# Gate product, sum and statistics of the attention block by halves in earlier slots, x's statistics four slots later

## The chip, the cores and the metric

The kernel runs on one core of one Trainium2 chip. The metric is the device time of one execution in microseconds, as the median of several runs.

## What is computed

Sixteen graphs of 512 tokens with 256 features go through one attention layer and one expert layer, both with a residual. Cut to what matters here:

```
x = x + gnn(layernorm(x), adj)        # statistics of x
x = x + ffn(layernorm(x))             # statistics of x1
gnn(x):  q, k, v = x Wq', x Wk', x Wv'            # 8 heads of 32
         c = softmax(where(adj, q k' / sqrt(32), -inf)) v
         gate = sigmoid([c, x] Wg' + bg)
         return gate * x + (1 - gate) * c
ffn(x):  two of 8 experts by the router's top 2, plus one shared expert
```

With z = tanh of half the gate's argument, gate is (z + 1)/2, so the layer's output is x1 = x + c + 0.5 (z + 1)(xn - c), where xn is the normalised x. The kernel computes `diff` = xn - c and x1 = x + c on GpSimd, then on VectorE the *gate product* diff = (z + 1) * diff and the *sum* x1 = 0.5 * diff + x1. x1's statistics follow, then its normalisation for the expert layer.

## The kernel before

**Stages.** The attention block goes through the 16 graphs (batches), software-pipelined over three of them: while batch b is in attention, b + 1 is normalised and projected ("pre") and b - 1 is gated and finished ("post"); b - 2 is routed ("late"). A program of 32 slots makes a batch. In each slot every engine has one score tile (128 queries of one head by 512 keys): TensorE computes the scores (L480), VectorE adds the mask and takes the maximum into `pf` and `nmax` (L836), one slot later ScalarE takes the exponent (L609), three slots later TensorE transposes it (L490), four later ScalarE copies it to `pt` (L597), and twelve slots later, for eight tiles together, TensorE multiplies with v (L511).

**Units.** Beside the tiles, `UNIT_AT` (L24) gives TensorE a unit of other work in a slot: V0, V1 (values), C0, C1 (transposes of the attention's output `c_tok`), R0 (router positions), Z0 to Z3 (gate, one of the four token tiles of 128 each), P0, P1 (transposes of the normalised xn), Q and K (projections), X0, X1 (transposes of the normalised x1). ScalarE evacuates the unit's high part in the next slot, VectorE the low part a slot after that (`low`: L697 for P, L700 for Q and K, L702 for C, L708 for V). Z units are evacuated by ScalarE alone, a tanh into a quarter of `z`.

**Order.** Every engine's order is written out by these tables and is static. `DVE_AT` (L29) sets VectorE's slots for the rest: `stat` and `var` are the four statistics of x and their aggregation (L732, L738, L740), `gate` is the gate product (L875), `x1` the sum (L880), `stat2` (two token tiles in the slot named and two in the next) and `var2` the same for x1. `POOL_AT` sets GpSimd's: `diff` and `x1` in slots 8 and 10, x's reciprocal deviation and normalisation in 12 and 13 (L936, L941), and from slot 17 on eight indirect DMAs (L923) that scatter batch b - 2 to the experts' rows. SP's queue stores the normalised xn (L370) and then x1 (L376), and then sends the stacks of q and k for the next scores.

**Waits that matter.** Scores have two banks, `S`, so those of slot p wait until VectorE is done with tile p - 2. Transposes wait for the exponent of their own tile and for the copy of two tiles before. Z0 to Z3 wait for both low parts of C before their second half. GpSimd's normalisation waits for `var`'s result `vr` on VectorE, and its scatters stand behind that in its queue.

**Behind the attention.** From the last batches on, TensorE interleaves the slots with the shared expert's blocks (`seam`); then come 35 routed blocks.

Of the kernel before, what the change touches and what calls it, by code (L numbers as in the profile page):

```python
# [12 lines left out]
ALU = mybir.AluOpType  # L13
# [12 lines left out]
HALVES = "QKV"  # L26

ACT_AT = {"exp": 5}
DVE_AT = {"choose": 3, "mark": 4, "weigh": 6, "place": 14, "stat": 8, "var": 12, "bias0": 4, "bias1": 16, "gate": 19,  # L29
          "x1": 20, "stat2": 21, "var2": 23}  # L30
POOL_AT = {"diff": 8, "x1": 10, "rstd": 12, "xn": 13, "rstd2": 24, "xn2": 25}
SCATTER_AT = {17: [0, 1], 18: [2, 3], 19: [4], 20: [5], 21: [6], 22: [7]}

# [32 lines left out]
def attention_phase(nc, sems, held, banks, x, adj, wqkv, wgate, bg, router_w, xn_dram, x1_dram, xt2_dram, xg_dram,  # L66
# [7 lines left out]
    NB, N, D = x.shape  # L74
# [18 lines left out]
    if True:  # L93
# [171 lines left out]
        def unit(b, name):  # L265

            return (b + 1) * NU + ORDER.index(name)
# [38 lines left out]
        def sync(sp):  # L306
# [53 lines left out]
            def end(b):  # L360
                par, att, pre, post = flags(b)
                B = b + 1
                A = b - 1
                if pre:
                    sp.wait_ge(s_bias, B * 2 + 1)
                    sp.dma_start(adj_i[:, :, :], (adj_t[B] if isinstance(B, int) else
                                 adj_t[bass.ds(B, 1)].rearrange("o p i n -> p (o i) n"))[:, 2:4]).then_inc(s_adj, 16)
                    if not first(b):
                        sp.wait_ge(s_xn, B * NT + NT)
                        sp.dma_start(xn_t[B] if isinstance(B, int) else  # L370
                                     xn_t[bass.ds(B, 1)].rearrange("o p i d -> p (o i) d"),
                                     xn[:, :, :]).then_inc(s_xnst, 16)
                if post:
                    dyn = not isinstance(A, int)
                    sp.wait_ge(s_mix, A * 2 + 2)
                    sp.dma_start(x1_t[bass.ds(A, 1)].rearrange("o p i d -> p (o i) d")  # L376
                                 if dyn else x1_t[A], x1[:, :, :]).then_inc(s_st, 16)
                if pre:
                    if att:
                        sp.wait_ge(s_full, b * POS + 16)  # L380
                        sp.nop().then_inc(s_held_sp, 1)
                    refs(B, unit(b, "K0") + 1, range(0, GRP, 2) if first(b) else range(GRP))
                    if first(b):
                        sp.wait_ge(s_xn, NT)
                        sp.dma_start(xn_t[0], xn[:, :, :]).then_inc(s_xnst, 16)
# [242 lines left out]
        def vector(dve):  # L628
# [57 lines left out]
            def low(b, par, name):  # L686

                B, A = b + 1, b - 1
                o = bank(b, name)
                k = int(name[1])  # L690
                if name[0] in "PQKC":
                    dve.wait_ge(g_hi, hi_index(b, name) + 1)
                else:
                    dve.wait_ge(g_full, unit(b, name) + 1)
                dve.wait_ge(g_free, unit(b, name))
                if name[0] == "P":
                    dve.tensor_tensor(xt_l[par][:, k, :], o[:, :], f32(xt_h[par][:, k, :]), ALU.subtract).then_inc(g_free, 1)  # L697
                elif name[0] in "QK":
                    hi, lo = (QH, QL) if name[0] == "Q" else (KH, KL)
                    dve.tensor_tensor(qk[:, k, lo, :], o[:, :], f32(qk[:, k, hi, :]), ALU.subtract).then_inc(g_free, 1)  # L700
                elif name[0] == "C":
                    dve.tensor_tensor(ct_l[:, k, :], o[:, :], f32(ct_h[:, k, :]), ALU.subtract).then_inc(g_free, 1)  # L702
                elif name[0] == "V":

                    if not isinstance(b, int) or b >= 1:
                        dve.wait_ge(pv, b * 4)
                        dve.nop().then_inc(s_held_dve, 1)
                    dve.tensor_copy(v[:, 2 * k:2 * k + 2, :, :].rearrange("p i h d -> p (i h) d"),  # L708
                                    o[:, :].rearrange("p (j d) -> p j d", d=DK)).then_inc(g_free, 1)
                elif name[0] == "X":  # L710
                    dve.wait_ge(s_mix, A * 2 + 1)
                    dve.nop().then_inc(s_held_dve, 1)
                    dve.tensor_copy(zf[:, N * k:N * k + N], o[:, :]).then_inc(g_free, 1)
                elif name[0] == "R":
                    dve.tensor_tensor(posb[:, :, :], o[:, 0:NT * E].rearrange("p (i e) -> p i e", e=E),
                                      start_e[:, :].rearrange("p (o e) -> p o e", o=1).to_broadcast([P, NT, E]),
                                      ALU.add).then_inc(g_free, 1)
# [104 lines left out]
            def at(b, p):  # L822
# [45 lines left out]
                if pre and p in (DVE_AT["bias0"], DVE_AT["bias1"]):  # L868

                    scores_mask(b, par, 0 if p == DVE_AT["bias0"] else 1)  # L870
                if post and p == DVE_AT["gate"]:

                    dve.wait_ge(g_free, unit(b, "Z3") + 1)
                    dve.wait_ge(s_d, A * 2 + 2)
                    dve.scalar_tensor_tensor(out=df[:, :], in0=zf[:, :], scalar=1.0, in1=df[:, :],  # L875
                                             op0=ALU.add, op1=ALU.mult).then_inc(s_mix, 1)
                if post and p == DVE_AT["x1"]:
                    dve.wait_ge(s_mix, A * 2 + 1)
                    x1f = x1[:, :, :].rearrange("p i d -> p (i d)")
                    dve.scalar_tensor_tensor(out=x1f, in0=df[:, :], scalar=0.5, in1=x1f,  # L880
                                             op0=ALU.mult, op1=ALU.add).then_inc(s_mix, 1)
                if post and p in (DVE_AT["stat2"], DVE_AT["stat2"] + 1):
                    second = p - DVE_AT["stat2"]
                    dve.wait_ge(s_mix, A * 2 + 2)
                    statistics(x1, stats2, s_stat2, A * (2 * NT + 1), (2 * second, 2 * second + 1))
                if post and p == DVE_AT["var2"]:
                    dve.wait_ge(s_xn2, A * NT)
                    variance(stats2, mv2, vr2, s_stat2, A * (2 * NT + 1))
# [11 lines left out]
        def pool(pool):  # L900
# [26 lines left out]
            def at(b, p):  # L927
# [15 lines left out]
                if post and p in (POOL_AT["diff"], POOL_AT["x1"]):  # L943

                    pool.wait_ge(s_norm, A * 2 + 2)
                    pool.wait_ge(s_xp, A * 32 + 32)
                    if p == POOL_AT["diff"]:
                        pool.wait_ge(s_mix, A * 2)
                        pool.tensor_tensor(diff[:, :, :], xnp[:, :, :], c_tok[:, :, :],
                                           ALU.subtract).then_inc(s_d, 1)  # L950
                    else:
                        pool.wait_ge(s_st, A * 32)
                        pool.wait_ge(s_xn2, A * NT)
                        pool.tensor_tensor(x1[:, :, :], xp[:, :, :], c_tok[:, :, :],
                                           ALU.add).then_inc(s_d, 1)
# [851 lines left out]
```

## Time and profile before

| what | value |
|---|---|
| median of 3 runs | 1925.34 us (1923.04 to 1927.98) |
| the profiled execution | 1923.95 us, span 1922.2 us |
| mean granted TensorE clock | 0.968 of full |
| TensorE matmul busy | 1765.3 us, 92% |
| VectorE busy | 1274.3 us, 66% |
| ScalarE busy | 1104.5 us, 57% |
| GpSimd busy | 672.8 us, 35% |

Busy shares are averages over the attention part (to about 1000 us) and the expert part. Times of a row are microseconds from the span's start. A matmul's end is modelled, so distances between starts say more than idle times beside them. Some matmul records are missing from a trace.

### The profile page before, as it was taken

What the parts mean: (1) busy time and instruction counts of PE and PEld (TensorE: products, weight loads), DVE (VectorE), ACT (ScalarE), POOL (GpSimd) and SP (SyncE); (2) the same over time, 40 slices, a digit from 0 to 9 for tenths busy, and PEclk for the clock granted to TensorE, in tenths of its full rate; (3) what the DMA queues carried; (4) which work ended last, traced back from release to release, by engine and by line L of the source; (5) the groups of instructions that cost most, each with busy time, mean ns of one, the idle gap of its engine ahead of it and who ended that gap; (6) DMA issues with size and microseconds to landing.
All of it is one profiled execution on the core that took longest, in us unless ns stands there. A gap on an engine that the chain in (4) does not pass through costs nothing. (4 is left out here: it accounts for less than half of the span.)

```text
span 1922.2 us, 36029 instructions
## 1 busy us (share of the span) xinstructions
PE 1765.3 (92%) x12613; PEld 1468.7 (76%) x12613; DVE 1274.3 (66%) x3155; ACT 1104.5 (57%) x2509; POOL 672.8 (35%) x512
## 2 busy tenths in 40 slices
PE   5899999988999888999889996989999999999996
PEld 4677777667777667777577885878989898898986
DVE  5676666766767766766645552467777777777773
ACT  4888778877778877778623331324444444444342
POOL 0125534335534335443221133003434343443334
PEclk8999999999999999999889996999999999999999
DMA  5445455544455544455213343245656565555553
GB/s 151 133 135 143 130 165 158 151 133 136 133 168 156 148 142 128 138 166 165 100 56 121 104 148 113 90 157 150 174 144 168 148 176 144 166 154 163 156 154 39
DMA packets 141329, 269.19 MB, mean 140 GB/s; under 512 B 15456, under 2 KB 92640, under 8 KB 136160
## 3 DMA queue, kind: packets, MB, share of 16 engines
q1 hardware_dynamic: 112608, 226.19, 38.3%
q0 software_dynamic: 28128, 39.93, 9.8%
q8 instruction: 102, 1.67, 0.4%
q10 hardware_dynamic: 416, 0.79, 0.2%
q14 instruction: 75, 0.61, 0.1%
HBM read 141.99 MB, written 74.52 MB: 113 GB/s over the span
## 5 line engine op out<-in xcount | busy, mean ns | idle before, releaser
L836 DVE CUSTOM_DVE_ANT_0 pf<-bank,bias_q 128x512 f32<-128x512 f32 x512 | 348.3, 687 | 268.6 <-PE bank L480 238.5
L1196 POOL DMA_INDIRECT out_x<-yb,ix x142 | 245.5, 1729 | 498.8 <-ACT yb L1414 408.0
L609 ACT ACTIVATE pf<-pf,nmax 128x512 f32<-128x512 f32 x512 | 371.8, 726 | 49.5 <-DVE nmax L836 49.5
L1426 ACT ACTIVATE ah<-am 128x512 fp32r<-128x512 f32 (+1 forms) x220 | 133.1, 605 | 440.8 <-DVE am L1494 434.8
L490 PE MATMUL bank<-ident,pf 128*128 128x128 f32 x2048 | 315.1, 276 | 55.5 <-issue 29.2
L1327 PE MATMUL bank<-xh,wl 128*128 128x512 f32 (+1 forms) x880 | 336.1, 382 | 6.0 <-issue 6.0
L490 PEld LDWEIGHTS bank<-ident,pf 128*128 128x128 f32 x2048 | 252.6, 142 | 115.3 <-issue 68.2
L1325 PE MATMUL bank<-xh,wh 128*128 128x512 f32 (+1 forms) x880 | 337.6, 384 | 3.2 <-issue 2.3
L1326 PE MATMUL bank<-xl,wh 128*128 128x512 f32 (+1 forms) x880 | 336.0, 382 | 2.0 <-issue 1.9
L597 ACT ACTIVATE pt<-bank 128x512 f32<-128x512 f32 x512 | 304.9, 596 | 13.9 <-PE bank L490 13.8
L480 PE MATMUL bank<-stack 96*128 96x512 f32 x512 | 237.2, 464 | 35.2 <-DMA stack<-qk 18.0
L1497 DVE TENSOR_TENSOR al<-am,ah 128x512 fp32r<-128x512 f32 (+1 forms) x220 | 146.7, 667 | 147.6 <-ACT ah L1426 144.8
L1325 PE MATMUL bank<-wh,ah 128*128 128x256 f32 x824 | 236.3, 287 | 3.5 <-issue 3.5
L1327 PE MATMUL bank<-wh,al 128*128 128x256 f32 x824 | 233.6, 283 | 3.6 <-issue 3.5
L1326 PE MATMUL bank<-wl,ah 128*128 128x256 f32 x824 | 233.2, 283 | 1.7 <-issue 1.7
L1494 DVE TENSOR_TENSOR am<-sg,bank 128x512 f32<-128x512 f32 (+1 forms) x220 | 143.0, 650 | 110.1 <-PE bank L1327 104.3
L1327 PEld LDWEIGHTS bank<-xh,wl 128*128 128x128 f32 x880 | 167.2, 190 | 39.3 <-issue 6.4
L1325 PEld LDWEIGHTS bank<-xh,wh 128*128 128x128 f32 x880 | 167.6, 190 | 38.3 <-issue 8.0
L1424 ACT ACTIVATE sg<-bank 128x512 f32<-128x512 f32 (+1 forms) x220 | 124.5, 566 | 121.0 <-PE bank L1327 88.8
L1326 PEld LDWEIGHTS bank<-xl,wh 128*128 128x128 f32 x880 | 167.7, 191 | 33.1 <-issue 2.6
L923 POOL DMA_INDIRECT xg_dram<-xn,idx x128 | 129.6, 1012 | 119.5 <-DVE idx L820 76.6
L480 PEld LDWEIGHTS bank<-stack 96*128 96x128 f32 x512 | 98.0, 192 | 88.8 <-issue 36.7
(213 smaller groups left out, 3202.3 us busy)
## 6 DMA issues: line engine op xcount, KB each, us to landing
raw<-in_w_all SPq DMA_DIRECT2D x39, 1536.0 KB, 7.3
stack<-qk SPq DMA_DIRECT2D x378, 128.0 KB, 2.4
xb<-xg_dram SPq DMA_DIRECT2D x32, 520.0 KB
adj_i<-in_adj SPq DMA_DIRECT2D x32, 512.0 KB, 5.1
xn<-in_x SPq DMA_DIRECT2D x16, 512.0 KB, 6.3
xn_dram<-xn SPq DMA_DIRECT2D x16, 512.0 KB
xp<-in_x SPq DMA_DIRECT2D x16, 512.0 KB, 6.7
xnp<-xn_dram SPq DMA_DIRECT2D x16, 512.0 KB, 7.6
```

The lines of the kernel that those rows point to most:

```text
L480: pe.matmul(S[p % 2][:, :], stack[0:SR, hd, 0, P * tq:P * tq + P], stack[0:SR, hd, 1, :], start=True, stop=True).then_inc(s_full, 1)
L490: last = pe.transpose(T[ep % 2][:, P * kt:P * kt + P], pf[ep % RING][:, P * kt:P * kt + P], ident[:, :])
L597: act.activation(pt[r][:, j, :, P * (tq % 2):P * (tq % 2) + P], T[ep % 2][:, :].rearrange("p (k q) -> p k q", q=P), ACT.Copy).then_inc(t_f ...
L609: act.activation(pf[i][:, :], pf[i][:, :], ACT.Exp, bias=nmax[:, i:i + 1], scale=-1.0, accum_out=den[:, g, tq, j:j + 1]).then_inc(p_exp, 1)
L836: dve.tensor_tensor_reduce(pf[r][:, :], S[p % 2][:, :], bias_q[1 - par][:, tq, :], -SCALE, -3.0 * MASKED, ALU.add, ALU.min, nmax[:, r:r + ...
L1196: pool.indirect_dma_start(out=out, out_offset=bass.IndirectOffsetOnAxis(ap=ix[n % RING][:, i:i + 1], axis=0), in_=yb[s][:, i, :], in_offse ...
L1325: pe.matmul(out_, lh, rh, start=first, stop=False)
L1326: pe.matmul(out_, lh, rl, start=False, stop=False)
L1327: return pe.matmul(out_, ll, rh, start=False, stop=last)
L1426: act.activation(ah[s][:, m, 0:cols], am[m % 2][:, 0:cols], ACT.Copy).then_inc(s_ah, 1)
L1494: dve.tensor_tensor(am[m % 2][:, 0:cols], sg[m % 2][:, 0:cols], UB[m % 2][:, 0:cols], ALU.mult).then_inc(s_am, 1)
L1497: dve.tensor_tensor(al[s][:, m, 0:cols], am[m % 2][:, 0:cols], f32(ah[s][:, m, 0:cols]), ALU.subtract).then_inc(s_al, 1)
```

## The change

It changes one table and the code that reads it. x's statistics move from slot 8 to slot 12, ahead of their aggregation. Gate product, sum and x1's statistics are issued for two token tiles (512 of 1024 elements per partition) at a time: gate product in slots 17 and 19, sum in 18 and 20, statistics in 19 and 21. The first half waits for unit Z1 in place of Z3. The semaphore `s_mix` counts four per batch in place of two, and who waits for it waits for the new counts.

```diff
-DVE_AT = {... "stat": 8, "var": 12, ... "gate": 19,
-          "x1": 20, "stat2": 21, "var2": 23}
+DVE_AT = {... "stat": 12, "var": 12, ... "gate": (17, 19),
+          "x1": (18, 20), "stat2": (19, 21), "var2": 23}
...
-                    sp.wait_ge(s_mix, A * 2 + 2)
+                    sp.wait_ge(s_mix, A * 4 + 4)
...
-                    dve.wait_ge(s_mix, A * 2 + 1)
+                    dve.wait_ge(s_mix, A * 4 + 3)
...
-                if post and p == DVE_AT["gate"]:
-
-                    dve.wait_ge(g_free, unit(b, "Z3") + 1)
-                    dve.wait_ge(s_d, A * 2 + 2)
-                    dve.scalar_tensor_tensor(out=df[:, :], in0=zf[:, :], scalar=1.0, in1=df[:, :],
-                                             op0=ALU.add, op1=ALU.mult).then_inc(s_mix, 1)
...
+                for half in range(2):
+                    hs = slice(half * NT * D // 2, (half + 1) * NT * D // 2)
+                    if post and p == DVE_AT["gate"][half]:
+
+                        dve.wait_ge(g_free, unit(b, "Z3" if half else "Z1") + 1)
+                        dve.wait_ge(s_d, A * 2 + 2)
+                        dve.scalar_tensor_tensor(out=df[:, hs], in0=zf[:, hs], scalar=1.0, in1=df[:, hs],
+                                                 op0=ALU.add, op1=ALU.mult).then_inc(s_mix, 1)
+                    if post and p == DVE_AT["x1"][half]:
+                        dve.wait_ge(s_mix, A * 4 + 2 * half + 1)
...
+                    if post and p == DVE_AT["stat2"][half]:
+                        dve.wait_ge(s_mix, A * 4 + 2 * half + 2)
+                        statistics(x1, stats2, s_stat2, A * (2 * NT + 1), (2 * half, 2 * half + 1))
...
-                        pool.wait_ge(s_mix, A * 2)
+                        pool.wait_ge(s_mix, A * 4)
```

VectorE in slots 8 to 13 of a batch, before. `pf` is the score tile's buffer (its number is the slot modulo 8), `v` the evacuation of V0 and V1, `ct_l` that of C0 and C1:

```order
L708 COPY v<-bank7 128x512
L732 BN_STATS stats<-xn 128x6 x4
L836 ISA pf1,nmax<-bank1,bias_q1 128x512
...
L836 ISA pf4,nmax<-bank0,bias_q1 128x512
L836 ISA nmax 128x1
L702 TENSOR_TENSOR ct_l<-bank6,ct_h 128x512
L738 BN_AGGR mv<-stats 128x2 x4
L740 TENSOR_SCALAR vr<-mv 128x4
L836 ISA pf5,nmax<-bank1,bias_q1 128x512
```

The same slots in the change:

```order
L708 COPY v<-bank7 128x512
L836 ISA pf1,nmax<-bank1,bias_q1 128x512
...
L836 ISA pf4,nmax<-bank0,bias_q1 128x512
L836 ISA nmax 128x1
L702 TENSOR_TENSOR ct_l<-bank6,ct_h 128x512
L732 BN_STATS stats<-xn 128x6 x4
L738 BN_AGGR mv<-stats 128x2 x4
L740 TENSOR_SCALAR vr<-mv 128x4
L836 ISA pf5,nmax<-bank1,bias_q1 128x512
```

The four statistics have left the place before tile 9 and stand before the aggregation, ahead of tile 13.

VectorE in slots 19 to 22, before (`xt_l0` is the evacuation of P0 and P1):

```order
L836 ISA pf3,nmax<-bank1,bias_q1 128x512
L836 ISA nmax 128x1
L875 SCALAR_TENSOR_TENSOR diff<-z,diff 128x1024
L836 ISA pf4,nmax<-bank0,bias_q1 128x512
L836 ISA nmax 128x1
L697 TENSOR_TENSOR xt_l0<-bank7,xt_h0 128x512
L880 SCALAR_TENSOR_TENSOR x1<-diff,x1 128x1024
...
L697 TENSOR_TENSOR xt_l0<-bank5,xt_h0 128x512
L732 BN_STATS stats2<-x1 128x6 x2
L836 ISA pf6,nmax<-bank0,bias_q1 128x512
L836 ISA nmax 128x1
L732 BN_STATS stats2<-x1 128x6 x2
```

Slots 17 to 20 in the change:

```order
L877 SCALAR_TENSOR_TENSOR diff<-z,diff 128x512
L836 ISA pf2,nmax<-bank0,bias_q1 128x512
L836 ISA nmax 128x1
L882 SCALAR_TENSOR_TENSOR x1<-diff,x1 128x512
L836 ISA pf3,nmax<-bank1,bias_q1 128x512
L836 ISA nmax 128x1
L732 BN_STATS stats2<-x1 128x6 x2
L877 SCALAR_TENSOR_TENSOR diff<-z,diff 128x512
L836 ISA pf4,nmax<-bank0,bias_q1 128x512
L836 ISA nmax 128x1
L697 TENSOR_TENSOR xt_l0<-bank7,xt_h0 128x512
L882 SCALAR_TENSOR_TENSOR x1<-diff,x1 128x512
```

Half of the gate product, the sum and the statistics now stand ahead of tile 20; slot 21 keeps one pair of statistics, slot 22 has none.

## Rows read from the trace of the kernel before

**Rows 1.** Waits of TensorE, whole run: total us, times, longest.

```profile
PE bank L490 <- issue: 29.2, 13, 2.6
PE bank L480 <- DVE nmax L836: 12.4, 21, 1.9
```

**Rows 2.** Order of time, VectorE, b = 6, slots 8 to 13: start, us, what.

```profile
374.22 0.69 DVE L708 COPY v<-bank 128x512 f32<-128x512 f32 x1
374.82 1.40 DVE L732 BATCH_NORM_STATS2 stats<-xn 128x6 f32<-128x256 f32 x4
376.14 0.67 DVE L836 CUSTOM_DVE_ANT_0 pf<-bank,bias_q 128x512 f32<-128x512 f32 x1
...
380.33 0.17 DVE L740 TENSOR_SCALAR vr<-mv 128x4 f32<-128x4 f32 x1
382.26 0.69 DVE L836 CUSTOM_DVE_ANT_0 pf<-bank,bias_q 128x512 f32<-128x512 f32 x1 [1.75 <-PE bank L480]
```

**Rows 3.** Order of time, TensorE, the same stretch.

```profile
375.74 0.60 PE L400 MATMUL bank<-ident,c_tok 128*128 128x128 f32 x4
376.87 0.51 PE L480 MATMUL bank<-stack 96*128 96x512 f32 x1 [0.54 <-DVE nmax L836]
377.22 0.60 PE L490 MATMUL bank<-ident,pf 128*128 128x128 f32 x4
377.65 0.60 PE L400 MATMUL bank<-ident,c_tok 128*128 128x128 f32 x4
378.01 0.48 PE L480 MATMUL bank<-stack 96*128 96x512 f32 x1
378.78 0.63 PE L490 MATMUL bank<-ident,pf 128*128 128x128 f32 x4 [0.29 <-ACT pt L597]
...
379.67 1.93 PE L511 MATMUL bank<-pt,v 128*32 128x256 f32 x32
```

**Rows 4.** Order of time, TensorE, slot 11 of b = 1 and of b = 14.

```profile
92.69 0.51 PE L480 MATMUL bank<-stack 96*128 96x512 f32 x1 [0.54 <-DVE nmax L836]
...
841.02 0.50 PE L480 MATMUL bank<-stack 96*128 96x512 f32 x1 [0.56 <-DVE nmax L836]
```

**Rows 5.** Order of time, TensorE, slots 18 to 21 of b = 1, 2 and 6.

```profile
107.32 0.60 PE L400 MATMUL bank<-ident,xn 128*128 128x128 f32 x4
...
111.95 0.50 PE L480 MATMUL bank<-stack 96*128 96x512 f32 x1
...
161.13 0.60 PE L400 MATMUL bank<-ident,xn 128*128 128x128 f32 x4
...
168.16 0.50 PE L480 MATMUL bank<-stack 96*128 96x512 f32 x1
...
391.82 0.60 PE L400 MATMUL bank<-ident,xn 128*128 128x128 f32 x4
...
397.42 3.52 PE L511 MATMUL bank<-pt,v 128*32 128x256 f32 x32
400.87 0.50 PE L480 MATMUL bank<-stack 96*128 96x512 f32 x1
```

**Rows 6.** Order of time, GpSimd, first and last of eight scatters, b = 6.

```profile
386.88 1.08 POOL L923 DMA_INDIRECT xg_dram<-xn,idx  x1 [0.18 <-issue]
...
396.10 0.96 POOL L923 DMA_INDIRECT xg_dram<-xn,idx  x1 [0.30 <-issue]
```

**Rows 7.** Stretch: us, busy PE, PEld, DVE, ACT, POOL, granted clock, DMA share, GB/s.

```profile
398.00:400.00 2.00, 2.00 (x27) 0.85 (x23) 1.29 (x4) 1.50 (x3) 0.00 (x0) 0.50 0.03 4
```

**Rows 8.** Order of time, VectorE, gate product of b = 6.

```profile
396.42 1.22 DVE L875 SCALAR_TENSOR_TENSOR diff<-z,diff 128x1024 f32<-128x1024 f32 x1
```

**Rows 9.** Order of time, all engines, slots 22 to 27, b = 6.

```profile
404.07 0.75 DVE L732 BATCH_NORM_STATS2 stats<-x 128x6 f32<-128x256 f32 x2
...
407.55 0.72 ACT L609 ACTIVATE pf<-pf,nmax 128x512 f32<-128x512 f32 x1 [0.25 <-DVE nmax L836]
...
409.48 0.63 PE L490 MATMUL bank<-ident,pf 128*128 128x128 f32 x4 [0.73 <-ACT pt L597]
```

## What the change was forecast to do

> **What bounds the kernel now.** I read the waits of TensorE first. Two sums matter here: 12.4 us in which scores wait for VectorE's `nmax`, and 29.2 us under "issue", for which the view names no engine [rows 1]. Then I read one steady batch, b = 6, on VectorE and TensorE in order of time, from slot 8 to slot 13 [rows 2, 3]. VectorE evacuates V0, then runs the four statistics of x, and only then, at 376.14, the score tile of slot 9. TensorE may not issue the scores of slot 11 before tile 9 is done, so it waits there, and waits again before the transposes of slot 12, because the exponent and the copy behind it on ScalarE are late too. The same pair of gaps stands in every batch from b = 1 to b = 14: 14 pairs, the first and last given [rows 4]. Just behind it, during the product with v, VectorE sits idle for 1.75 us [rows 2].
>
> The next thing to see is the hold in slots 19 to 21. In b = 1, where GpSimd scatters nothing, the scores behind the second product start 4.63 us after the transposes of P0 (107.32 to 111.95). In b = 2 it is 7.03 us (161.13 to 168.16), in b = 6 it is 9.05 us (391.82 to 400.87) [rows 5]. The hold begins about 5 us after GpSimd's first scatter and ends near its last [rows 6]. In its wake the granted clock is 0.50, that is 1.2 GHz, and the 32 matmuls of the product take 3.52 us in place of 1.93 [rows 3, 5, 7]. The gate product of 1.22 us lies inside this hold on VectorE [rows 8].
>
> Behind the hold VectorE and ScalarE catch up: the second pair of x1's statistics (slot 22) pushes the later score tiles back; ScalarE waits 0.25 us for `nmax` at 407.55, and TensorE 0.73 us for ScalarE at 409.48 [rows 9].
>
> **The change part by part.**
>
> *x's statistics out of slot 8.* VectorE's tile 9 starts at 374.82 in place of 376.14, 1.32 us earlier. What TensorE gets: undisturbed, scores follow a unit's first transpose by 0.36 us (377.65 to 378.01), so the scores at 376.87 would start at 375.74 + 0.36 = 376.10, 0.77 earlier. The transposes at 378.78 would follow their scores, which stand at 378.01, by 0.35 as at 377.22, and so come 0.42 earlier again. Together 1.19 us [rows 3]. The idle time printed beside the two rows, 0.54 + 0.29 = 0.83, is the lower bound (ends of matmuls are modelled), the 1.32 us of VectorE the upper. Over 14 batches: 1.19 x 14 = **16.7 us**, bounds 11.6 and 18.5.
>
> *The same statistics into slot 12.* They stand now between ct_l of C0 and the aggregation. TensorE runs its product of 1.9 us there. Tile 12 and ct_l come 0.77 us earlier with their scores, the statistics add 1.32, so `vr` starts at 380.33 - 0.77 + 1.32 = 380.88 and ends at 381.05. The scores of slot 13 come 1.19 us earlier, and tile 13 can start at 382.26 - 1.19 = 381.07 [rows 2]. The cover, 1.75 us of idle time, is just used up. Cost 0. If it falls short, tile 13 and ct_l of C1 behind it are late, and Z0 on TensorE waits for ct_l; at most half of the 1.32 us, since Z0's first matmuls don't read it: 0.7 x 14 = 10 us.
>
> *GpSimd.* It waits for `vr`, which lands 0.55 us later than now, normalises xn and then scatters. xn is ready before the first scatter, now at 386.88, then at 387.43; P0 needs it at 391.82 - 1.19 = 390.63, so 3 us are left. The scatters start 0.55 us later in time and 1.74 us later measured on TensorE's progress [rows 2, 5, 6]. SP's queue stores xn, then x1; the first comes 0.55 later, the second earlier. Nobody waits for either in this batch.
>
> *Gate product and sum by halves.* Four instructions of 512 elements replace two of 1024. A 1024 one takes 1.22 us [rows 8]; a 512 one on VectorE takes 0.69, but the next instruction starts 0.60 after it (374.22 to 374.82) [rows 2]. So the split costs VectorE nothing to 0.16 us for each of two, in stretches where it is idle: the first half in slot 17 and its sum in slot 18 need only Z1, `diff` and GpSimd's x1, all long there. Cost 0; if all of it lay on the path, 0.32 x 15 = 5 us. The Trainium skill ("VectorE: DVE Perf Modes", section "The TRN2 errata — SBUF-src ops pay a fixed extra latency per instruction") speaks against the split: a fixed cost per instruction, paid once by a large tile, and a two-input fp32 time of (N + 151)/0.96 ns, hence 157 ns more for each split. The durations agree with it (0.69 and 1.22 us), the starts show most of it overlapped; by the page the sum would be 5 us smaller.
>
> *x1's statistics in slots 19 and 21 in place of 21 and 22.* Slot 19's pair takes the room that the gate product leaves: a pair of statistics takes half of the 1.32 us above, so 0.66 + 0.60 against 1.22. Slot 22 is rid of its pair, 0.66 us, at 404.07 [rows 9]. Tiles 23 and 24 come up to 0.66 earlier. After that ScalarE is the one that is late, with 0.25 us of waiting to gain and no more, plus a few hundredths; TensorE follows it at 409.48. I take 0.3 us for 14 batches: **4 us**, bounds 0 and 0.66 x 14 = 9. Late next: ScalarE's chain of exponent and copy.
>
> *The hold, under a shifted schedule.* TensorE arrives with P0 and P1 before the hold instead of in it. No row shows this. The nearest from one side is b = 2, where P0 escaped: 7.03 against 9.05, a gain of 2.0 us per batch; from the other, everything stays as it is and the scatters' 0.55 us are added. Twelve batches (b = 3 to 14), so 24 us less to 7 us more. Since b = 2 is one batch, I take a quarter of it, 0.5 x 12 = **6 us** of gain.
>
> Sum: 16.7 + 4 + 6 = 27 us. The profiled execution ran 1923.95 us (span 1922.2, 1.75 around it); less 27 gives 1897. It lies 1.4 us under the median of the three runs, 1925.34, so the forecast is **1898 us**. The chain of work that ended last lies in the expert part behind, and runs over TensorE's matmuls; TensorE's order there is fixed, so time won before it stays won.
>
> **Rivals.**
>
> *The hold falls under the product.* It is tied to the scatters in time; TensorE by then has the product's 1.93 us, the next scores and their transposes to do, which need no answer from another engine at once, and since it isn't idle the clock stays at 1.00. For: in b = 2 the matmuls of the product ran on within the hold. Against: only one batch looks so. Of the hold's price, 9.05 - 4.63 = 4.4 us, at least b = 2's 2.0 would go and at most all; with the middle, 3.2: 1925 - 21 - 12 x 3.2 = **1866**.
>
> *The release decides, not the arrival.* If TensorE goes on only when the scatters are over, and gets no credit for what it did before, the loop runs from the release over slot 12 to the scatters and back; the scatters now lie later in it by 0.55 us, slot 22 gives 0.3 back. 1925 + 13 x 0.25 = **1928**, no difference. For it: GpSimd's start is the only thing that the change makes later. Against it: TensorE's rows inside the hold show work issued.
>
> *Slower.* The same loop, and the halves of gate product and sum in slots 17 and 18, which now run beside the scatters, delay GpSimd's descriptors. Price: 0.69 us for each of two, 13 batches, 18 us: **1946**. It decides from the point where a scatter's pitch exceeds 1.26 us. Against it: the gate product at 396.42 overlapped the scatter at 396.10, which took its usual 0.96 us [rows 6, 8]. The Trainium skill ("SBUF — State Buffer", section "Who interferes with whom") has such a rule, that a VectorE instruction with two SBUF inputs contends with a GpSimd one that reads SBUF; this trace doesn't show it for the scatters.
>
> *Slot 12 is too full.* The cover is short by 0.7 us: 1898 + 10 = **1908**, faster still.
>
> **How the numbers follow.** Forecast 0.58 (its own range 1885 to 1906), hold under the product 0.18, slot 12 too full 0.07, release decides 0.11, slower 0.06. A measurement of this kernel tells about 0.3%, 5.8 us, from no change. Faster: 0.58 + 0.18 + 0.07 = 0.83; within 0.3% 0.11; slower 0.06. The range leaves out the last two and the far end of the first rival: 1870 to 1914.
>
> **What would show it.** Right: no `nmax` wait of TensorE in slot 11 and none of 0.29 behind it; `nmax` waits fall from 12.4 us to under 6; tile 9 follows V0's copy by 0.60; `vr` of x within 0.2 us of tile 13; first scatter 1.7 us nearer to P0 than the 4.94 us now. The distance from P0 to the scores behind the product tells the hold: 9.05 as now, about 8.5 as forecast, under 7 for the first rival. Wrong: a wait for ct_l before Z0, a longer pitch of scatters, or the whole unchanged although both gaps are gone.

## The result, and the profile after

| | before | changed |
|---|---|---|
| median, same chip | 1926.42 us (1923.04 to 1932.9, 6 runs) | 1912.63 us (1908.87 to 1916.36, 6 runs) |
| ratio | | 0.9927, 95% interval 0.9913 to 0.9942 |
| profiled execution | 1923.95 us, span 1922.2 | 1910.72 us, span 1909.0 |
| mean granted TensorE clock | 0.968 | 0.969 |

Faster, by half of what was forecast: 14 us in place of 27. The range 1870 to 1914 holds the value; its centre does not.

The waits of TensorE, in the kernel after: engine, line waited for, then us in total, times, longest. The `nmax` wait of scores has gone from 12.4 us [rows 1] to 2.5. The nameless wait that stood at the transposes L490 [rows 1] now stands mostly at the product, L511.

```profile
PE bank L511 <- issue: 18.9, 29, 1.1
...
PE bank L490 <- issue: 8.6, 18, 1.0
...
PE bank L480 <- DVE nmax L836: 2.5, 3, 1.9
```

VectorE in order of time, b = 6, slots 8 to 13, after; compare [rows 2].

```profile
373.28 0.69 DVE L708 COPY v<-bank 128x512 f32<-128x512 f32 x1
373.88 0.68 DVE L836 CUSTOM_DVE_ANT_0 pf<-bank,bias_q 128x512 f32<-128x512 f32 x1
...
378.18 1.40 DVE L732 BATCH_NORM_STATS2 stats<-xn 128x6 f32<-128x256 f32 x4
379.71 0.38 DVE L738 BATCH_NORM_AGGREGATE mv<-stats 128x2 f32<-128x6 f32 x4
380.12 0.17 DVE L740 TENSOR_SCALAR vr<-mv 128x4 f32<-128x4 f32 x1
380.31 0.69 DVE L836 CUSTOM_DVE_ANT_0 pf<-bank,bias_q 128x512 f32<-128x512 f32 x1
```

TensorE, the same stretch; compare [rows 3].

```profile
374.79 0.60 PE L400 MATMUL bank<-ident,c_tok 128*128 128x128 f32 x4
375.15 0.48 PE L480 MATMUL bank<-stack 96*128 96x512 f32 x1
...
376.26 0.48 PE L480 MATMUL bank<-stack 96*128 96x512 f32 x1
376.66 0.63 PE L490 MATMUL bank<-ident,pf 128*128 128x128 f32 x4
```

Tile 9 follows the copy of V0 by 0.60 us. The scores of slot 11 follow C0's transposes by 0.36 (1.13 before), the transposes of slot 12 follow their scores by 0.40 (0.77 before). Both gaps are gone. The idle time of VectorE before tile 13 is used up: tile 13 comes 0.19 behind `vr`, and does not hold TensorE up, since P0 comes 1.16 us earlier after C0 than before.

TensorE in slots 18 to 22 of b = 6, after; compare [rows 5].

```profile
389.71 0.60 PE L400 MATMUL bank<-ident,xn 128*128 128x128 f32 x4
...
392.48 2.19 PE L511 MATMUL bank<-pt,v 128*32 128x256 f32 x29
395.70 0.38 PE L511 MATMUL bank<-pt,v 128*32 128x256 f32 x1 [1.03 <-issue]
396.42 0.38 PE L511 MATMUL bank<-pt,v 128*32 128x256 f32 x1 [0.35 <-issue]
397.18 0.38 PE L511 MATMUL bank<-pt,v 128*32 128x256 f32 x1 [0.38 <-issue]
397.48 0.50 PE L480 MATMUL bank<-stack 96*128 96x512 f32 x1
397.82 0.27 PE L490 MATMUL bank<-ident,pf 128*128 128x128 f32 x1
398.60 0.49 PE L490 MATMUL bank<-ident,pf 128*128 128x128 f32 x3 [0.51 <-issue]
```

GpSimd, the same batch: normalisation, then first and last two of the eight scatters; compare [rows 6].

```profile
381.61 5.18 POOL L942 TENSOR_SCALAR xn<-xn,mv,rstd 128x256 f32<-128x256 f32 x4 [0.21 <-POOL rstd L937]
386.97 1.09 POOL L924 DMA_INDIRECT xg_dram<-xn,idx  x1 [0.18 <-issue]
...
394.97 1.09 POOL L924 DMA_INDIRECT xg_dram<-xn,idx  x1 [0.31 <-issue]
396.37 0.96 POOL L924 DMA_INDIRECT xg_dram<-xn,idx  x1 [0.30 <-issue]
```

The hold is there as before, and it now falls where TensorE is inside the product. About from the start of the seventh scatter to 1.3 us behind the end of the last, TensorE goes on by one instruction or two each 0.7 us: the last three matmuls of the product start at 395.70, 396.42 and 397.18, where elsewhere one follows another by 0.06. From P0 to the scores behind the product it is 7.77 us (389.71 to 397.48) in place of 9.05, but the hold reaches on into the transposes behind.

b = 6 is one of the cheap batches, though. In four of the 13 batches with a hold (b = 6, 8, 11 and 13) the granted clock stays at 1.00 through the hold and behind it. In the other nine it falls to 0.50, that is 1.2 GHz, from 7.7 to 9.2 us after P0 on. Stretch of b = 7 (columns as in [rows 7]) and TensorE in it; the four transposes of a tile, 0.60 us at a clock of 1.00, take 1.01:

```profile
454.50:457.50 3.00, 2.93 (x11) 2.56 (x11) 2.43 (x6) 2.48 (x5) 0.00 (x0) 0.50 0.07 24
```

```profile
454.57 1.01 PE L490 MATMUL bank<-ident,pf 128*128 128x128 f32 x4 [0.60 <-issue]
```

To see whether it became shorter, a batch is cut in three at fixed matmuls: first C0 transpose, P0 (the first transpose of `xn` in slot 18), X0 (the first of x1's `xn2`, unit X0 in slot 29), next C0. The table has the means over b = 2 to 14, worked out from the starts of those matmuls in order of time. Without any hold P0 to X0 takes 17.62 to 17.66 us, and 17.25 to 17.28 with x1's statistics by halves (see the experiments); "hold" is what is above that.

| kernel (chip) | C0 to P0 | P0 to X0 | hold | X0 to C0 | batch |
|---|---|---|---|---|---|
| before (first) | 16.08 | 21.87 | 4.25 | 19.94 | 57.89 |
| changed (first) | 14.92 | 22.24 | 4.99 | 19.85 | 57.00 |

So 1.16 us per batch were won ahead of P0, and P0 to X0, which should have become shorter, became 0.37 longer. If x1's statistics give the 0.37 us here that they give without a hold, the hold took 0.74 back; that they do is assumed in this split and not shown. By batch, P0 to X0 is 21.1 to 21.2 us in the four where the clock stays up (22.1 in the same b = 6 before) and 22.0 to 23.8 in the nine where it falls. Before, the clock falls in 11 of the 13. So the clock has a part in both sizes of the hold, and no run separates it. The span agrees with the table: C0 of b = 2 and of b = 15 start, before, at 145.05 and 897.63, and after, at

```profile
143.68 0.38 PE L400 MATMUL bank<-ident,c_tok 128*128 128x128 f32 x2
...
884.68 0.49 PE L400 MATMUL bank<-ident,c_tok 128*128 128x128 f32 x3
```

That is 1.4 us gained by b = 2, 11.6 over 13 batches, and 0.3 behind: 13.2 us, all of the difference of the spans.

### The profile page after: what moved, and what is told of

Its sections match the earlier page's. It is cut to its first block and busy times, and to the rows that moved or that the text cites. A ratio compares the mean times of both kernels' runs of the same rounds, so it can differ in the third digit from the quotient of the medians.

```text
span 1909.0 us, 36077 instructions
## 1 busy us (share of the span) xinstructions
PE 1767.9 (93%) x12613; PEld 1479.1 (77%) x12613; DVE 1281.3 (67%) x3187; ACT 1107.5 (58%) x2509; POOL 680.2 (36%) x512
## 5 line engine op out<-in xcount | busy, mean ns | idle before, releaser
L490 PE MATMUL bank<-ident,pf 128*128 128x128 f32 x2048 | 322.8, 279 | 27.0 <-ACT pt L597 18.1
L490 PEld LDWEIGHTS bank<-ident,pf 128*128 128x128 f32 x2048 | 257.1, 143 | 88.2 <-issue 41.1
L1326 PEld LDWEIGHTS bank<-wh,ah 128*128 128x128 f32 x824 | 155.7, 189 | 6.4 <-issue 5.8
```

The lines of the kernel that those rows point to most:

```text
L490: last = pe.transpose(T[ep % 2][:, P * kt:P * kt + P], pf[ep % RING][:, P * kt:P * kt + P], ident[:, :])
L1326: pe.matmul(out_, lh, rh, start=first, stop=False)
```

## The experiments

The experiments ran in five groups, each on one chip with the kernel before beside them, and the groups were of unequal kind; this is the main finding. In three the kernel before takes 1837 to 1839 us and the profiled kernels show no hold in slots 19 to 21; in two it takes 1906 to 1907, with a hold (the first comparison, at 1926, is of that kind too). Each ratio is to the kernel before on the same chip. Which kind a group met was not chosen. The chips of the five are numbered 14, 11, 5, 3 and 14 on record, and number 14 has no hold in the first group and a hold in the fifth, 40 minutes later. If the number names one chip both times, the hold comes and goes on a chip; "a chip with the hold" below means no more than a chip as it was in that group.

### Chips without the hold

**x's statistics in slot 12 alone** (kernel before otherwise).

```diff
-"stat": 8, "var": 12,
+"stat": 12, "var": 12,
```

> Only x's statistics move, from slot 8 to slot 12; gate product, sum and x1's statistics stay whole in slots 19 to 22. Theory A (the hold costs by when the scatters end, and later scatters eat part of the gain): C0 to P0 falls from 16.08 to about 14.9 us in every batch, as with both moves; the distance from P0 to X0 grows by about half a microsecond; the whole is 9 to 12 us faster than before (1915 us). Rival B (the halves are what eats the gain, by running beside the scatters): this one alone gives the whole 17 us, 1909 us or less, and the hold is as before.

Measured: 1822.6 us against 1838.06, ratio 0.9912 (0.9888 to 0.9936). Per batch C0 to P0 14.95, P0 to X0 17.66. P0 to the scores behind the product is 4.64 in every batch: nothing to be held.

**The halves alone** (changed kernel, statistics back in slot 8).

```diff
-"stat": 12, "var": 12,
+"stat": 8, "var": 12,
```

> Only gate product, sum and x1's statistics are issued by halves in slots 17 to 21; x's statistics stay in slot 8. Theory A: C0 to P0 stays 16.08 us, scatters and hold stay where they were, and slot 22's relief gives 0.3 us per batch: 3 to 5 us faster than before, 1922 us. Rival B (the halves delay the scatters): first to last scatter takes longer than 10.2 us, and the whole is slower than before by 5 us or more.

Measured: 1831.84 us, 0.9963 (0.9949 to 0.9976). C0 to P0 16.10, P0 to X0 17.25: 0.4 us per batch from x1's statistics and nothing lost by the split.

**x's statistics in slot 11** (changed kernel otherwise).

```diff
-"stat": 12, "var": 12,
+"stat": 11, "var": 12,
```

> The changed kernel with x's statistics in slot 11 in place of 12 (before tile 12 and the low part of C0). VectorE is without idle time there but for 0.17 and 0.32 us, so the variance can come some 0.5 us earlier, and the scatters behind it on GpSimd too. Theory A (the release from the hold follows the scatters in time): 0.3 to 0.5 us per batch faster than the changed kernel, 4 to 6 us in all, 1907 us. Rival C (the hold's extra cost has another cause than the later scatters): within 2 us of the changed kernel, 1912.

Measured: 1816.43 us, 0.9874 (0.9846 to 0.9901). The same as the changed kernel gives below: slot 11 or 12 makes no difference.

**All scatters behind tile 22** (changed kernel; before a batch's first scatter GpSimd waits until VectorE has finished 23 tiles of the batch, the last of them tile 22).

```diff
                     for j in SCATTER_AT[p]:
+                        if j == 0 and b < NB:
+                            pool.wait_ge(s_done, b * POS + 23)
                         scatter(b - 2, j)
```

> The changed kernel, but GpSimd's first scatter of a batch waits until VectorE is done with score tile 22 (batches below 16). Theory A (the hold belongs to the scatters): P0 to the scores behind the product takes 4.6 us in every batch as in b = 1, the granted clock stays 1.00 there, and the hold appears 5 us and more after the new start, near slots 26 to 31; X0 comes late because GpSimd normalises x1 only behind the scatters; the whole is slower. Rival D (the hold belongs to the place in TensorE's order, the transposes of P0 and P1 and the product behind the gate's matmuls): the hold stays in slots 19 to 21.

Measured: 1966.29 us, in one run. GpSimd's normalisation of x1 now stands behind the scatters, and TensorE waits for it in each batch. GpSimd, then TensorE, in order of time:

```profile
430.53 0.96 POOL L924 DMA_INDIRECT xg_dram<-xn,idx  x1 [0.30 <-issue]
...
434.99 4.84 POOL L967 TENSOR_SCALAR xn<-x,mv,rstd 128x256 f32<-128x256 f32 x4 [2.43 <-DMA xg_dram<-xn,idx]
```

```profile
439.98 1.08 PE L400 MATMUL bank<-ident,xn 128*128 128x128 f32 x4 [9.77 <-POOL xn L967]
```

It bounds how late the scatters may be, and as this chip has no hold it says nothing on the hold.

The two parts were run again, on two other such chips, in the hope of a chip with the hold.

> Kernel before with x's statistics in slot 12 alone, once more, in the hope of a chip that shows the hold (kernel before at 1906 or 1926). It is this part that puts the scatters 1.0 us later against the first C0 transpose while TensorE comes 1.2 us earlier. If the hold grows by that, this kernel gains less than its 1.18 x 14 = 16.5 us: on a chip like that of the last runs about nothing (0.998 to 1.000), on one like the first 0.9955. If the halves are to blame for what the change lost, it gains its 16.5 us in full: 0.991. Without a hold 0.991 by either.

> Changed kernel with x's statistics back in slot 8. The scatters stand where they stood in the kernel before, so the hold should too, and the 0.38 x 14 = 5.3 us of x1's statistics should be gained in full: ratio 0.997, with or without a hold. If the halves on DVE lengthen the scatters or their wait, it is 1.000 or above on a chip with the hold.

Measured: 0.9900 (0.9874 to 0.9926) and 0.9962 (0.9948 to 0.9976), kernel before 1836.79 us. Once more, with the changed kernel beside them:

> The changed kernel itself. Without the hold (kernel before at about 1838): 1.18 x 14 + 0.38 x 14 = 22 us less, ratio 0.988. With it (1906 or 1926): 0.998 or 0.993 again. If it stands at 0.993 or above without the hold too, the parts hinder each other and the hold is not what took the gain.

> Kernel before with x's statistics in slot 12 alone. With the hold: near 1.000 if the later scatters lengthen it, 0.991 if the halves are to blame. Without: 0.991.

> Changed kernel with x's statistics in slot 8. With the hold: 0.997 if the scatters' time against TensorE sets it, 1.000 or above if the halves lengthen it. Without: 0.997.

Measured: changed kernel **1815.89 us against 1838.94, ratio 0.9875** (0.9857 to 0.9893); the parts 0.9908 (0.989 to 0.9925) and 0.996 (0.9949 to 0.9972). The parts add up, -0.0092 and -0.0040 to -0.0125, that is 23 us. The forecast without its term on the hold was 21. The rows of b = 6 in the changed kernel, TensorE, slots 18 to 21: the scores follow P0 by 4.64 us and no matmul waits.

```profile
369.71 0.60 PE L400 MATMUL bank<-ident,xn 128*128 128x128 f32 x4
...
372.49 1.93 PE L511 MATMUL bank<-pt,v 128*32 128x256 f32 x32
374.35 0.50 PE L480 MATMUL bank<-stack 96*128 96x512 f32 x1
```

GpSimd there: the scatters have the same pitch as on the first chip.

```profile
375.23 0.96 POOL L924 DMA_INDIRECT xg_dram<-xn,idx  x1 [0.30 <-issue]
376.49 0.96 POOL L924 DMA_INDIRECT xg_dram<-xn,idx  x1 [0.30 <-issue]
```

### Chips with the hold

The **changed kernel** and the **kernel before**, both with a profile of their own.

> The changed kernel itself, with a profile, beside a run of the kernel before on the same chip. On a chip that shows no hold in slots 19 to 21 (kernel before about 1838 us, P0 to the first product matmul 2.77 us in every batch) the two terms alone should count: 1.18 x 14 + 0.38 x 14 = 22 us, so 1816 us, ratio 0.988. On a chip that shows the hold (kernel before about 1926) it should come to 1912 again, ratio 0.993: the hold takes back about 0.65 us a batch. A rival, that the halves and the moved statistics hinder each other whatever the hold does, says 0.993 on both.

> The kernel before with a profile of its own on this chip, to lay the two chips side by side. Without the hold: 14 batches of about 53.5 us from one first C0 transpose to the next, C0 to P0 16.08, P0 to product 2.77, product to scores 1.86. With it: 57 to 58.7 us, P0 to product 5.5 to 6.0, product to scores 2.9 to 3.6. If the 86 us between the chips are the hold alone, the sum of the P0-to-scores stretches carries all of it (4.2 x 12 = 50 us at most from the trace of the kernel before), and the rest has to lie in the stretch behind the last attention batch or in the clock.

Measured: 1902.8 us against 1906.04, ratio **0.9977** (0.996 to 0.9993); the kernel before against itself 0.9989 (0.9971 to 1.0007), which shows how far such a ratio can be trusted. Here all but some 4 of the 22 us are lost. TensorE's wait under "issue" at the transposes L490, kernel before, then changed kernel:

```profile
PE bank L490 <- issue: 5.4, 10, 1.8
```

```profile
PE bank L490 <- issue: 13.6, 33, 1.1
```

TensorE within the hold, b = 6, kernel before: the product runs on, at 2.43 us for 1.93, and one set of transposes waits. The granted clock stays at 1.00 from P0 to X0 in all 13 batches here, where it fell in 11 on the first chip; hold 2.10 us and not 4.25.

```profile
386.77 2.43 PE L511 MATMUL bank<-pt,v 128*32 128x256 f32 x32
389.13 0.50 PE L480 MATMUL bank<-stack 96*128 96x512 f32 x1
390.03 0.60 PE L490 MATMUL bank<-ident,pf 128*128 128x128 f32 x4 [0.40 <-issue]
```

Changed kernel: the end of the product and the transposes behind it go one by one. The clock falls in 6 of its 13 batches; P0 to X0 is 20.9 to 21.0 us in the other seven and 21.4 to 21.8 in the six.

```profile
386.43 2.73 PE L511 MATMUL bank<-pt,v 128*32 128x256 f32 x31
389.53 0.38 PE L511 MATMUL bank<-pt,v 128*32 128x256 f32 x1 [0.37 <-issue]
390.21 0.39 PE L480 MATMUL bank<-stack 96*128 96x512 f32 x1 [0.30 <-issue]
390.95 0.42 PE L490 MATMUL bank<-ident,pf 128*128 128x128 f32 x2 [0.35 <-ACT pf L609]
...
392.35 0.27 PE L490 MATMUL bank<-ident,pf 128*128 128x128 f32 x1 [0.38 <-issue]
```

**Kernel before, first scatter held until the mark of slot 17.**

```diff
                     for j in SCATTER_AT[p]:
+                        if j == 0 and b < NB:
+                            pool.wait_ge(s_done, b * POS + 18)
                         scatter(b - 2, j)
```

> Kernel before, its first scatter held until the mark of slot 17, all eight some 2 us later than its progress gives. If later scatters against TensorE lengthen the hold, this kernel loses 0.5 to 1.2 us a batch, 7 to 17 us, on a chip with the hold. If the hold falls where the scatters leave it and later only shifts it: 0. Where there is no hold: 0, unless xn2's normalisation comes late.

Measured: 1904.54 us, 0.9994 (0.9975 to 1.0013), no difference in time. In the trace the hold has moved with the scatters, from slots 19 to 21 into slots 22 to 24: P0 to the scores behind the product is 4.63 again in every batch, and the hold per batch is 3.08 us against 2.10 (the clock falls in 5 of the 13 batches, and in none of the kernel before on this chip). In the profiled executions the 13 batches are 12.9 us longer by that, but the expert part is 7.0 us shorter and the start 1.0, and the median shows nothing; whether lateness by itself costs time is thus not settled by the times. That the hold follows the scatters is. The rows show who is held: VectorE and ScalarE wait too, on nothing that the view can name, and TensorE then for them. VectorE, ScalarE, TensorE, b = 6:

```profile
399.27 0.69 DVE L836 CUSTOM_DVE_ANT_0 pf<-bank,bias_q 128x512 f32<-128x512 f32 x1 [1.90 <-remote]
```

```profile
399.20 0.60 ACT L546 ACTIVATE qk<-bank 128x512 fp32r<-128x512 f32 x1 [1.65 <-remote]
```

```profile
400.02 0.51 PE L480 MATMUL bank<-stack 96*128 96x512 f32 x1 [1.62 <-DVE nmax L836]
```

**Scatters a slot apart** (changed kernel). Scatter j waits until VectorE has finished 16 + j tiles of the batch, the last of them tile 15 + j.

```diff
                     for j in SCATTER_AT[p]:
+                        if b < NB:
+                            pool.wait_ge(s_done, b * POS + 16 + j)
                         scatter(b - 2, j)
```

> Changed kernel, scatter j of a batch waits for the DVE's mark of slot 16+j, so that the eight lie a slot (about 2.2 us) apart instead of 1.26. If the hold comes from GpSimd issuing scatters back to back, it shrinks where it is present and the time falls by up to 3 us x 12; where it is absent nothing is to be gained, and the later end of the scatters (about 8 us) delays xn2's normalisation: up to 5 us a batch, +70 us, as scatters behind tile 22 did with 10 us a batch. If the end of the scatters still lies ahead of x1's variance (slot 23), it is +0.

Measured: **1850.12 us, 0.9704** (0.9679 to 0.9729). Only the last three scatters come later than in the changed kernel, by 0.5, 2.1 and 2.6 us after C0, and the hold is 0.87 us per batch in place of 3.99. Nothing was lost by the later end: the last scatter ends 0.8 us before `vr` of x1 is ready. GpSimd, b = 6:

```profile
379.92 0.96 POOL L924 DMA_INDIRECT xg_dram<-xn,idx  x1 [1.88 <-DVE nmax L836]
381.78 0.96 POOL L924 DMA_INDIRECT xg_dram<-xn,idx  x1 [0.90 <-DVE nmax L836]
383.58 1.05 POOL L961 TENSOR_TENSOR rstd<-vr,mhalf 128x4 f32<-128x4 f32 x1 [0.84 <-DVE vr L740]
```

**The same on the kernel before**, on two chips without the hold and then on one with it.

> Kernel before with scatter j held until the mark of slot 16+j, as in the spread kernel. On a chip with the hold: if pace is what makes it, it falls here too, about 1.7 to 3 us x 13, and the time comes to some 1870 us where the kernel before has 1906; and between this kernel and the spread one (1850) lie again the 22 us of the two terms. If the spread kernel gained for another reason (the change's own slots), nothing or a loss. Without a hold: 1.000.

> Kernel before with the scatters a slot apart. With the hold: it falls to some 0.981 of the kernel before if the scatters' pace makes it, 1.000 if the spread kernel owed its gain to the change's own slots. Without: 1.001, as measured on such a chip.

> Kernel before with the scatters a slot apart. With the hold: some 0.981 of the kernel before if the scatters' pace makes it, 1.000 if the spread kernel owed its gain to the change's own slots. Without: 1.000.

Measured: 1.0016 (1.0003 to 1.0029) and 0.9997 (0.9987 to 1.0006) without the hold; with it **1866.42 us, 0.9796** (0.9779 to 0.9814), hold 0.24 us per batch. So the hold depends on the pace of the last scatters, in either kernel; later ones at the old pace, in the run from slot 17, kept it. Between 0.9796 and 0.9704 the change is worth about 17 us once its scatters are spread too (two groups, both kernels before within 1 us).

**Slot 12 alone, on a chip with the hold.**

> Kernel before with x's statistics in slot 12 alone. With the hold: near 1.000 if the later scatters lengthen it, 0.991 if the halves are to blame. Without: 0.991.

Measured: 1904.52 us, **0.9992** (0.9975 to 1.001), against 0.990 to 0.991 in three groups without the hold. This part by itself gives back all that it wins, and the halves are not needed for that. Its P0 to X0 is 21.43 us, where the kernel before has 19.73 on the second group's chip, and the clock falls in none of its 13 batches, so slow issue alone can take the gain back. The halves alone never ran on a chip with the hold. Between 0.9992 and 0.9977 they would keep about 3 us of their 5, and between P0 to X0 of 21.43 and 21.23 as much, but the two intervals overlap and the runs are of two groups, so this is not shown.

**Spread scatters and slot 11**, meant as the fastest.

> Changed kernel with the scatters spread and x's statistics in slot 11 in place of 12: vr comes some 0.5 us earlier, and with it the scatters. Without a hold statistics in slot 11 gave 6 us more than in 12 (1816.4; the change's own terms 22 below the kernel before). Expected 0.968 of the kernel before on a chip with the hold, 0.987 without, which would be the fastest of all; if slot 11's DVE work reaches tile 12 the gain is gone and it is at 0.970 or above.

Measured, on a chip without the hold: 1816.15 us, 0.9885 (0.9858 to 0.9912), no better than the changed kernel's 0.9875. The 6 us that the expectation gave to slot 11 compared kernels with and without the halves, which was a mistake. The version that beats both kernels is the changed one with spread scatters: 0.9704 with the hold; without it, the run nearest to it says 0.9885, as the change.

The means per batch, all on chips with the hold but the last two rows:

| kernel | 7th scatter behind C0 | C0 to P0 | P0 to X0 | hold |
|---|---|---|---|---|
| before | 19.1 | 16.09 | 19.73 | 2.10 |
| before, scatters from slot 17 | 23.9 | 16.09 | 20.70 | 3.08 |
| before, spread | 22.7 | 16.12 | 17.86 | 0.24 |
| slot 12 alone | 20.2 | 14.95 | 21.43 | 3.8 |
| changed | 20.2 | 14.92 | 21.23 | 3.99 |
| changed, spread | 22.2 | 14.98 | 18.11 | 0.87 |
| changed, no hold | 20.5 | 14.95 | 17.28 | 0 |
| slot 12 alone, no hold | 20.2 | 14.91 | 17.66 | 0 |

## Why the prediction was half right

*x's statistics out of slot 8*: right. 1.19 us per batch forecast, 1.16 measured with the hold, 1.18 without, and every row that was to show it does.

*The same statistics into slot 12, cost 0*: right for TensorE. The cover was just used up, and no wait for ct_l was added.

*GpSimd*: the direction was right and the size short. The first scatter is 12.18 us behind C0 (374.79 to 386.97) where it was 11.14; so 1.04 later and not 0.55. The aggregation waits 0.13 behind the statistics, `vr` starts 5.33 behind C0 in place of 4.59, and the normalisation takes 5.18 us; before it took:

```profile
381.82 4.88 POOL L941 TENSOR_SCALAR xn<-xn,mv,rstd 128x256 f32<-128x256 f32 x4 [0.21 <-POOL rstd L936]
```

The 0.30 us more are in the last of the four instructions. It now runs beside VectorE's making of a mask from `adj_i` (L672, slot 16), which started 1.26 us after the normalisation's end before (386.70 to 387.96), and takes 1.55 us where the other three take 1.22. GpSimd, then VectorE, after:

```profile
385.25 1.55 POOL L942 TENSOR_SCALAR xn<-xn,mv,rstd 128x256 f32<-128x256 f32 x1
```

```profile
385.85 0.69 DVE L672 TENSOR_SCALAR bias_q<-adj_i 128x1024 bf16<-128x1024 int32 x1
```

It is so in 12 of the 13 batches (1.35 in b = 4, where they overlap less), and with the statistics in slot 8 no batch shows it.

The lateness against P0 is 2.20 us (4.94 to 2.74), not 1.74. Costing this at nothing held only where there is no hold.

*Halves of gate product and sum, cost 0*: right. Nothing is missing from P0 to X0 in the runs of the halves, and the starts of the rows, which had the fixed cost overlapped, were the ones to go by: the next instruction starts 0.59 us after a gate half (378.72 to 379.31, halves alone) and 1.14 after the whole (376.00 to 377.14, slot 12 alone), without a hold. By an estimate from the Trainium skill ("VectorE: DVE Perf Modes", section "The TRN2 errata — SBUF-src ops pay a fixed extra latency per instruction") 5 us of the gain would have been missing; the runs of the halves show none of it. The slower rival did not come in the time, but what it rests on does show, at a smaller price: in the changed kernel without a hold, a scatter that starts 0.3 us into a gate half takes 1.23 us in place of 0.96, and the next follows it by 1.53 in place of 1.27. VectorE, then GpSimd:

```profile
368.06 0.69 DVE L877 SCALAR_TENSOR_TENSOR diff<-z,diff 128x512 f32<-128x512 f32 x1
```

```profile
368.36 1.23 POOL L924 DMA_INDIRECT xg_dram<-xn,idx  x1 [0.30 <-issue]
```

It is about 0.27 us at each of two scatters in nearly every batch, where the rival had 0.69, and TensorE waits for neither. With this the contention which the Trainium skill ("SBUF — State Buffer", section "Who interferes with whom") describes for two SBUF inputs agrees at the gate half. At the sum half, which has two as well, the scatter that starts with it takes 0.96. The kernel before had such a scatter too, the second, beside the one-input L672 (1.22 us).

*x1's statistics*: 0.3 x 14 = 4 us forecast, 0.37 measured without a hold, 5 us. With the hold it was not measured by itself.

*The hold, under a shifted schedule*: **this step failed.** It took 0.5 x 12 = 6 us of gain, and the first chip shows 0.74 x 13 = 10 us of loss by the split above; the bare lengthening of P0 to X0 is 0.37 x 13 = 5 us. It went wrong in its reading of b = 2. That P0 and the product escape the hold was taken for a part of the hold saved. The runs show a stretch tied to the last two or three scatters in time: whatever lies in it is issued slowly, and what escapes ahead only makes room for what comes next. Its price is what TensorE would else have done there. In the kernel before the seventh scatter comes 3 us behind P0, after the change 5.3. It now meets the end of the product and the transposes behind, many small instructions. That small instructions make it dear is read from the rows of b = 6 on both chips; it was not tried by itself. On the first chip the fall of the clock in nine batches comes on top, at another place than before. That the moved statistics alone are enough for the loss is shown by the run of slot 12 alone on a chip with the hold. The bound of 7 us on the side of loss was too narrow as well, if the split holds.

Two of the signs misled as well. "Under 7 for the first rival, about 8.5 as forecast" reads 7.77 in b = 6, a gain by that measure, while the hold had moved past the point at which it ends; only a cut as late as X0 sees all of it. And b = 6 is a batch that did gain, 21.15 us from P0 to X0 in place of 22.06, while the mean of the 13 lost; one batch could not tell. The rival "the hold falls under the product" came true in its place (the product is no longer run at 1.2 GHz as in [rows 7]) but not in its price: the product's matmuls are themselves held, and in nine batches the clock falls behind them instead. Of the 38 us that it gave to the hold nothing came.

The rival "the release decides, not the arrival" was the nearest in kind: the scatters' place in the loop sets when TensorE goes on. For a chip like that of the second group (0.9977) it is close to what happens. It fell short where it gave the arrival no credit at all: the first chip kept 14 of its 22 us.

What makes the hold stays open. It needs scatters close together (spread ones remove nine tenths of it in the kernel before and three quarters in the changed one), it isn't in every group with the same scatters at the same pitch, and it holds VectorE and ScalarE too. SP's stores of xn and x1 alone don't make it, since b = 1 has them, has no scatters and no hold. Longer transfers don't show: over b = 2 to 14 of the changed kernel the mean packet of a scatter takes 126 ns with the hold and 125 without, one of SP's queue 84 in both, and one that brings instructions 0.78 and 0.80 us with it, while the runs without it have 0.75 to 0.82. How long an instruction was awaited, the traces don't tell. Leaving half of the scatters out was not tried, as the experts would read rows that nobody wrote.

## What to carry to other kernels

A wait under "issue" that no engine explains is not a fixed cost at a place in the program; look for what runs beside it in time, here a burst of indirect DMAs, and ask of each moved step which of the two sides it moves. Before tuning around such a wait, spread the burst: one semaphore wait per scatter gave 2 to 3% where the hold was, more than the change itself, and nothing where it wasn't (1.0016 and 0.9997). And a gain that is measured on one chip may be another on the next or at another time, so read stretch by stretch, over all batches and not one, what it consists of.

## What the hardware showed that was not expected

The hold is a matter of the chip or its state, not of the program alone: the kernel before took 1926, 1906 and 1907 us with it and 1838, 1837 and 1839 without, and 1838 and 1907 are both of a chip numbered 14. No kernel before was profiled without the hold. The 70 us between the later groups lie in the batches (some 26 us by the profiled executions, 725.0 for b = 2 to 14 of the kernel before against 698.9 with the scatters spread and no hold) and, more of them, behind (from C0 of b = 15 to the end 1016 to 1028 us with it, 989 to 998 without). There it stands under the 32 padding scatters that GpSimd issues back to back. The stretch from first to last of them, changed kernel, first chip (busy us and instructions of TensorE, its weight loads, VectorE, ScalarE, GpSimd, granted clock, DMA share, GB/s):

```profile
1118.20:1158.70 40.50, 24.61 (x107) 18.59 (x106) 10.85 (x29) 5.96 (x10) 31.05 (x32) 0.73 0.50 164
```

and without the hold:

```profile
1050.10:1090.60 40.50, 40.50 (x226) 35.19 (x225) 22.13 (x46) 13.78 (x24) 31.06 (x32) 1.00 0.70 222
```

The same 32 scatters in the same 40.5 us, but 107 matmuls in place of 226, and VectorE and ScalarE at half of their work or less. The granted clock is 0.73 there, a mean between 2.4 and 1.2 GHz; how much of the price is the clock's is open. An estimate from the two counts, 119 matmuls too few at 0.18 us each, is 21 us, the largest piece in one place; no kernel here touched it.
